# Token lists of a mixture-of-experts layer inverted in two passes instead of one

## The reference, cut to what matters

```
x  = x + layernorm(attention(layernorm(x)))
xf = layernorm(x)                                   # 4096 x 256
probs = softmax(xf @ gate_w.T); topw, topi = top_k(probs, 2)
topw  = topw / topw.sum()
y  = ffn(xf, shared) + sum over e of ffn(xf, expert[e]) * weight of e (0 where e was not chosen)
x  = x + layernorm(y)
ffn(x, g, u, d) = (silu(x @ g.T) * (x @ u.T)) @ d.T  # g, u: 704 x 256; d: 256 x 704
```

## Time and profile before

| | us |
|---|---|
| median of 3 runs | 857.32 (856.37 to 857.96) |
| the profiled execution | 857.45 |
| its span in the trace | 855.7 |

### The profile page before, as it was taken

How to read it: one execution, slowest core, us unless ns; L and a number is a source line. 1 busy time by engine, 2 the same in 40 slices (tenths; PEclk the granted TensorE clock), 3 DMA queues, 4 the chain that set the end, 5 groups by cost and what they waited for, 6 DMA issues and landing times.

```text
span 855.7 us, 21069 instructions
## 1 busy us (share of the span) xinstructions
PE 786.6 (92%) x6583; PEld 643.3 (75%) x6592; DVE 586.6 (69%) x1591; ACT 484.8 (57%) x1068; POOL 291.6 (34%) x316
## 2 busy tenths in 40 slices
PE   6889999999999998666899999999999999999991
PEld 2447777777777776544788888888888888888880
DVE  6668889898988888894887444555555555555553
ACT  2264848485757675422566555565656565656562
POOL 3011010101010100062265555555555555555542
PEclk9999999999999999997999999999999999999996
DMA  4104334443535252502245545646463646464733
GB/s 191 50 25 179 112 142 112 152 125 144 145 121 152 101 156 74 148 1 71 50 68 77 100 76 73 123 76 145 72 148 70 148 69 148 68 146 68 147 42 96
DMA packets 102691, 90.10 MB, mean 105 GB/s; under 512 B 63760, under 2 KB 94224, under 8 KB 101456
## 3 DMA queue, kind: packets, MB, share of 16 engines
q1 hardware_dynamic: 87648, 68.45, 27.7%
q0 software_dynamic: 14976, 20.78, 16.0%
HBM read 48.70 MB, written 27.39 MB: 89 GB/s over the span
## 4 chain that ended last, share of the span: by engine, by line
PE 68%; DVE 17%; ACT 6%; issue 4%; DMA 3%; POOL 1%; ACTq 0%; SPq 0%; DVEq 0%; POOLq 0%
PE ps L911 39%; PE ps L926 18%; PE ps L991 3%; DVE wgu L1286 3%; PE ps L1023 3%; DVE hf L1226 2%; ACT wgu L771 2%; PE ps L985 2%; DVE wdn L1286 1%; DVE st L1402 1%; DVE st L1206 1%; DVE wdn L1535 1%; PE ps L952 1%; DVE hT L1236 1%; ACT silu L723 1%
## 5 line engine op out<-in xcount | busy, mean ns | idle before, releaser
L911 PE MATMUL ps<-xhl,wgu 128*128 128x256 f16 x3102 | 386.3, 274 | 13.1 <-DMA xhl<-attw 6.5
L911 PEld LDWEIGHTS ps<-xhl,wgu 128*128 (+1 forms) x3102 | 302.9, 98 | 57.6 <-issue 10.4
L1226 DVE SCALAR_TENSOR_TENSOR hf<-ps,sc,silu 128x256 f32<-128x256 f32 x330 | 159.6, 484 | 187.5 <-ACT silu L723 148.2
L926 PE MATMUL ps<-wdn,hT 128*128 (+1 forms) x1870 | 253.7, 274 | 11.3 <-DVE hT L1236 8.9
L723 ACT ACTIVATE silu<-ps,sc 128x256 f32<-128x256 f32 x275 | 130.4, 474 | 234.1 <-PE ps L911 211.4
L926 PEld LDWEIGHTS ps<-wdn,hT 128*128 128x128 f16 x1870 | 182.4, 98 | 37.1 <-DVE hT L1236 6.3
L672 POOL DMA_INDIRECT acc_d<-ysb,gst x78 | 129.2, 1657 | 44.5 <-POOL gst L668 30.9
L605 POOL TENSOR_TENSOR rstd<-ve,mhalf 128x4 f32<-128x4 f32 (+1 forms) x32 | 30.7, 960 | 297.5 <-DVE ve L1211 276.2
L1236 DVE TENSOR_TENSOR hT<-hf,hT 128x256 f16<-128x256 f32 x275 | 115.1, 418 | 1.7
L737 ACT CAST hT<-hf 128x256 f16<-128x256 f32 x275 | 109.8, 399 | 10.2 <-DVE hf L1226 8.4
L661 POOL DMA_INDIRECT attw<-xn_d,gst x78 | 80.4, 1031 | 44.5 <-POOL gst L657 32.6
(11 more groups left out here) (241 smaller groups left out, 775.2 us busy)
## 6 DMA issues: line engine op xcount, KB each, us to landing
wgu<-in_gu SPq DMA_DIRECT2D x8, 1408.0 KB, 6.0
att<-in_x SPq DMA_DIRECT2D x16, 512.0 KB, 5.5
wdn<-in_dn SPq DMA_DIRECT2D x8, 768.0 KB, 8.1
x_d<-att SPq DMA_DIRECT2D x8, 512.0 KB, 2.9
xn_d<-wgu SPq DMA_DIRECT2D x8, 512.0 KB, 3.3
acc_d<-ysb SPq DMA_DIRECT2D x16, 256.0 KB, 3.1
att<-x_d SPq DMA_DIRECT2D x8, 512.0 KB
att<-acc_d SPq DMA_DIRECT2D x7, 512.0 KB
```

Source lines behind the costliest of these rows:

```text
L911: ins = te.matmul(o, slot_gu(slot, hw, k, j), x(hx, k), start=(n == 0), stop=(n == len(TERMS) - 1))
L926: ins = te.matmul(y_bank(u, tt), h(hh), slot_dn(slot, c, hw), start=(c == 0 and n == 0 and tt == 0), stop=(c == FC - 1 and n == 1 and tt = ...
L1226: v.scalar_tensor_tensor(out=hf[lo:P, c % 2 * TW:(c % 2 + 1) * TW], in0=up, scalar=scale_of(slot, 1, lo, P), in1=silu[lo:P, c % 2 * TW:(c ...
```

## The change

The lists of the eight constant tiles (16 columns) are inverted first, in TAIL. The lists of the others (62 columns) are inverted in routed tiles 0 to 3: VectorE makes eight groups of column one-hots at the positions HOT_AT of the routed tiles' chunks, TensorE multiplies two chunks later, and `route_indices(1)` follows. A position is six times the tile plus the chunk.

- Every expert's list now starts at a fixed place, so that the 16 columns need no counts. Ranks come from matmuls over prefixes (`ranks`: 28 matmuls for the first 28 blocks, 11 for the last 4) in place of L1048, L1049 and the eight scans.
- Place one-hots (`one_lo`) are one instruction of 1024 columns for four blocks, all on VectorE, without the token's number; all eight groups are kept in `att`. Column one-hots (`one_hi`) are made by two instructions, a comparison and a product with the token's number: 896 and 128 columns for the first pass, 496 columns in each of eight groups for the second.
- `route_weights` is a step of its own; its first part moves behind `rows2` and `logits` of batch 7. `route_positions` is done in two parts.
- Counts, segments, `route_order` and `route_table` move behind the first pass's indices.
- SP stores the routing weights in two parts, and loads expert 8's weights after tile 4's transposes and the second pass's last matmul, since `att` holds the place one-hots till then. The preparation of expert 8 moves from positions 17 to 32 to positions 26 to 37.
- GpSimd waits for the second part of `idx` before the gather of tile 8; ScalarE and TensorE wait for `eid` before tile 8 and no longer before tile 0.

```
 LAST_ORDER: ("route_norm", 0) now ahead of ("route_top1", 0); ("route_weights", 0) behind ("logits",); ("route_slots", 0) ahead of ("D", 11)
+TAIL = [("G", 0), ("route_positions", 0), ("H", 0), ("route_norm", 1), ("G", 1), ("route_top1", 1), ("G", 2), ("H", 1), ("D", 0), ("route_top2", 1),
+        ("one_lo", 0), ("G", 3), ("H", 2), ("route_slots", 1), ("D", 1), ("route_weights", 1), ("one_lo", 1), ("one_hi", 0), ("G", 4), ("H", 3),
+        ("D", 2), ("invert", 0), ("route_positions", 1), ("one_lo", 2), ("one_lo", 3), ("invert", 1), ("G", 5), ("H", 4), ("D", 3), ("invert", 2),
+        ("one_lo", 4), ("one_lo", 5), ("invert", 3), ("invert", 4), ("G", 6), ("one_lo", 6), ("one_lo", 7), ("one_hi", 1), ("invert", 5),
+        ("invert", 6), ("invert", 7), ("route_indices", 0), ("H", 5), ("D", 4), ("route_counts",), ("G", 7), ("H", 6), ("D", 5),
+        ("route_segments",), ("G", 8), ("H", 7), ("D", 6), ("route_order",), ("G", 9), ("H", 8), ("D", 7), ("G", 10), ("H", 9), ("D", 8),
+        ("route_table",), ("G", 11), ("H", 10), ("D", 9), ("H", 11), ("D", 10), ("D", 11)]
+PREP_AT = ((0, 2, 4, 6, 7, 8, 9, 11, 13, 15), (26, 27, 28, 29, 30, 31, 32, 34, 35, 37))
+PREP_STEPS = (("max", 0), ("max", 1), ("max", 2), ("diag", 0), ("spread", 0), ("scale", 0), ("prep", 0), ("prep", 1), ("prep", 2), ("prep", 3))
+HOT_AT = (1, 3, 5, 10, 12, 14, 16, 18)
+LATE |= {divmod(at, FC): ("one_hi", 0, g) for g, at in enumerate(HOT_AT)}
+LATE |= {divmod(HOT_AT[-1] + 3, FC): ("indices", 0, 0)}
+INVERT_AT = {divmod(at + 2, FC): g for g, at in enumerate(HOT_AT)}
...
 # SP, in the loop over the routed tiles
+                if i == 5:
+                    sp.wait_ge(rest_used, OHG)
+                    sp.dma_start(last_gu, gu_in[E]).then_inc(last_loaded, 16)
+                    sp.dma_start(last_dn, dn_in[E]).then_inc(last_loaded, 16)
...
 # TensorE
+            def ranks(n):
+                t0, t1 = PART[n]
...
+                te.matmul(dst, upper16, m16[:, E * t0:E * t1], start=True, stop=False)
+                for b in range(PART_B[n][0]):
+                    te.matmul(dst.rearrange("p (t e) -> p t e", e=E), ones16[:, :], each(bsum16[:, E * b:E * b + E], t1 - t0), start=False, stop=False)
+                for t in range(t0, t1 - 1):
+                    ins = te.matmul(dst[:, E * (t + 1 - t0):].rearrange("p (t e) -> p t e", e=E), ones16[:, :], each(m16[:, E * t:E * t + E], t1 - 1 - t),
+                                    start=False, stop=(t == t1 - 2))
...
+            def invert(n, g):
+                pe.wait_ge(onehot_lo_made, g + 1)
...
+                for h in range(OHB):
+                    for m in range(2):
+                        hi = oh_first[:, m, OHB * g + h, :] if n == 0 else oh_rest[g % 2][:, m, h, :]
+                        ins = te.matmul(inverted(n), oh_lo[g][:, m, h, :], hi, start=(g == 0 and h == 0 and m == 0), stop=(g == OHG - 1 and h == OHB - 1 and m == 1))
+                ins.then_inc(rest_used if n else first_used, 1)
...
 # VectorE
+            def one_hi(dst, lo, hi, c0, c1, made):
+                shape = [P, 2, hi - lo, c1 - c0]
...
+                rl(v.tensor_tensor(dst, h4, c4, ALU.is_equal))
+                v.tensor_tensor(dst, dst, t4, ALU.mult).then_inc(made, 1)
+            def one_lo(g):
+                shape = [P, 2, OHB, P]
...
+                v.tensor_tensor(oh_lo[g], l4, i4, ALU.is_equal).then_inc(onehot_lo_made, 1)
```

More of the change, by code:

```diff
@@ L77 @@
[L77 to L82, removed]
@@ L204, in build @@
         last_gu, last_dn = att[:, 0:KD * GU], att[:, KD * GU:KD * GU + FC * D]
[L207 to L211, removed]
+        routes = wdn[:, (E - 1) * SLOT_DN:E * SLOT_DN].bitcast(F32)
+        r_p, r_t, r_o1, r_o2, r_c, r_x = (routes[:, NTB * E * n:NTB * E * (n + 1)] for n in range(6))
+        route_rest = spare[:, 2 * KD * S + 2 * NT * D:SLOT_GU].bitcast(F32)
@@ L221, in build @@
[L221 to L226, removed]
+        STATIC = E * TT
@@ L1026, in _ @@
                         ins.then_inc(att_done, 1)
+                if kind == "route_slots":
+                    ranks(step[1])
                 if kind == "turn2" and b in PE_SECOND:
@@ L1044, in _ @@
                 if kind == "route_slots":
-                    pe.wait_ge(m_made, 2)
-                    x2_ready(pe, B - 1)
-                    te.matmul(att_ps[0][:, 0:256], upper[:, :], r_m, start=True, stop=True)
-                    te.matmul(att_ps[0][:, 256:512], ones[:, :], r_m, start=True, stop=True).then_inc(counted, 1)
+                    ranks(step[1])
+                if kind == "route_counts":
+                    pe.wait_ge(logits_made, B)
+                    for b in range(B):
+                        ins = te.matmul(att_ps[3][:, E * b:B * E].rearrange("p (t e) -> p t e", e=E), ones16[:, :], each(bsum16[:, E * b:E * b + E], B - b),
+                                        start=(b == 0), stop=(b == B - 1))
+                    ins.then_inc(counted, 1)
                 if kind == "route_order":
@@ L1053, in _ @@
                 if kind == "invert":
-                    for h in range(OHB):
-                        j = OHB * step[1] + h
-                        pe.wait_ge(onehot_made, step[1] + 1)
-                        pe.wait_ge(onehot_lo_made, POOL_H * step[1] + max(1, h - (OHB - POOL_H) + 1))
-                        for m in range(2):
-                            ins = te.matmul(att_ps[1][:, 0:NCOL], oh_lo[step[1] % OHR][:, m, h, :], oh_hi[step[1]][:, m, h, :],
-                                            start=(j == 0 and m == 0), stop=(j == NTB - 1 and m == 1))
-                    ins.then_inc(onehot_used, 1)
-            pe.wait_ge(eid_made, 1)
+                    invert(0, step[1])
             def routed(i, r, slot, before, later=None):
@@ L1335, in route @@
                     first_of(o2, m2)
-                    v.tensor_tensor(mm, o1, o2, ALU.add).then_inc(m_made, 1)
+                    rl(v.tensor_tensor(mm, o1, o2, ALU.add))
+                    sums = bsum16[:, E * PART_B[n][0]:E * PART_B[n][1]]
+                    with nc.allow_low_precision(reason="whole numbers up to 4"):
+                        v.tensor_reduce(sums.rearrange("p (b e) -> p b e", e=E), mm.rearrange("p (b t e) -> p b e t", t=NT, e=E), AX.X, ALU.add).then_inc(m_made, 1)
+                if kind == "route_weights":
                     rl(v.tensor_tensor(ms, m1, m2, ALU.add))
@@ L1461, in _ @@
                     ffn_step(kind, step[1], 2 * B - 2, 0)
[L1462 removed]
+                if kind in ("route_norm", "route_top1", "route_top2", "route_weights", "route_positions"):
                     route(kind, step[1])
[L1464 to L1476 removed]
+                if kind == "one_lo":
+                    if step[1] == 0:
+                        dve.wait_ge(rows2_hi, B)
+                        dve.wait_ge(x2_stored, 16 * B)
+                    one_lo(step[1])
@@ new lines, in _ @@
+                if kind == "one_hi":
+                    if step[1] == 0:
+                        c3 = col16.rearrange("p (i h) -> p i h", h=TT)
+                        for h in range(TT):
+                            ins = v.tensor_scalar(c3[:, 0:E, h], expert_at, 1.0 / P, float(h), ALU.mult, ALU.add)
+                        rl(ins)
+                    one_hi(oh_first[:, :, PART[step[1]][0]:PART[step[1]][1], :], PART[step[1]][0], PART[step[1]][1], 0, STATIC, first_hi_made)
+                if kind == "route_indices":
+                    route_indices(0)
@@ L1577, in lay_out @@
                     prep(s, n, *stage)
+                if kind == "one_hi":
+                    wait(dve, rest_used, n - 1)
+                    one_hi(oh_rest[n % 2], OHB * n, OHB * (n + 1), STATIC, NCOL, rest_hi_made)
+                if kind == "indices":
+                    route_indices(1)
             def ml(ins, b, n):
```

230 lines of the change are left out of this document (129 added, 101 removed), and 6 rows, old and new, of the table LAST_ORDER.

## The result

| | before | after |
|---|---|---|
| median of 4 runs, us | 857.01 (856.37 to 857.96) | 864.6 (863.71 to 865.52) |
| profiled execution, us | 857.45 | 863.71 |
| its span, us | 855.7 | 861.9 |

The account below looks back on a forecast made before the run. DVE was taken to set the pace in the tail until the token lists stand, PE in the routed tiles. 857.45 - 5.8 (tail) + 3.5 (routed tiles) = 855.15, adjusted to the median: forecast 855.0 us, range 850 to 861.

Parts of the forecast that it names:

- The tail: From batch 7's end to tile 0's first matmul: tile 0 starts 5.8 us sooner, at 396.5, bounds 393.5 and 400.
- Rows ready earlier, tile 0 no longer waits: Start of tile 0: first lists at 379.1, rows at 388.9, PE's 6.5 us wait for transposed rows gone.
- I take 1.14 for `one_lo`: Place one-hots on DVE: 1.14 us per 1024-column instruction, one element a cycle; 0.55 or 1.4 were the alternatives.
- H7 at 383.2 to 383.9: Shared expert in the tail: DVE's step H7 was walked to run from 383.2 to 383.9 us, then order until 387.3.
- tile 0 starts at 396.5: End of the tail: PE free at 395.4, plus 1.1 us for slow matmuls; bounds 393.5 and 400.
- The walk: Step-by-step count of the tail along DVE's and PE's queues, giving tile 0's start.
- The point at 348.12 becomes 350.4: DVE's last softmax block in the tail: moving the weights' first part costs 2.15 us and one 0.1 us wait.
- Give-back 3.5, bounds 0.5 to 8: Routed tiles 0 to 6: second-pass matmuls and DVE stalls, less the cold start, lose 3.5 us net.
- the cold start: Tile 0's first 36 matmuls: following other work, they fall from 5.57 to 3.9 us, gaining 1.65.
- C: Rival, routed tiles 0 to 5: DVE overload makes PE wait, give-back 8 us, tail 1 us worse, 860.5; chance 0.2.
- D: Rival, tail: not shorter because PE runs slowly through most of it, tile 0 at 400, time 858.5; chance 0.13.
- Expert 8's load: 0, bounds 0 and 4: Weight load for expert 8, now starting at position 20.5, needed behind 26: costs 0 us, bounds 0 and 4.

Follow-up runs that it names:

- Number 3: The changed kernel with `route_order` moved ahead of H7 and D6 in the tail; 864.25 us, ratio 1.0065 to the kernel before.
- number 11: The changed kernel measured once more, unchanged, on another chip; 867.56 us, ratio 1.0117 to the kernel before.
- number 6: The changed kernel with the routing weights' first part back in its old place behind `route_top2`; 861.42 us, ratio 1.0043 to the kernel before.
- number 2: The changed kernel with both spreads, scale and pieces one chunk later; 861.7 us, ratio 1.0026 to the kernel before.
- number 5: The changed kernel with one of eight second-pass groups, expert 8's load kept at the changed kernel's place; 858.51 us, ratio 1.0013 to the kernel before.
- Number 1: The changed kernel with only the first of eight second-pass groups, which also released expert 8's load earlier; 865.82 us, ratio 1.0073 to the kernel before.
- 4: The changed kernel with 16 filler matmuls of 256 columns ahead of each of the two late spreads; 866.85 us, ratio 1.0073 to the kernel before.
- 8: The changed kernel with the edits of numbers 2, 3 and 6, plus 66 filler matmuls in the tail; 852.9 us, ratio 0.9949 to the kernel before.
- 9: Number 8 without its 66 filler matmuls; 851.71 us, ratio 0.994 to the kernel before.
- 10: Number 8 with `route_table` earlier, two second-pass one-hot groups made in the tail, the other six repositioned; 850.23 us, ratio 0.9913 to the kernel before.
- 7: The changed kernel with the edits of numbers 2 and 3 together; 854.68 us, ratio 0.996 to the kernel before.

## Why the prediction was wrong, step by step

Two terms of the sum failed. The tail was to gain 5.8 us and gained 3.0, most of that by luck; the routed tiles were to give back 3.5, at most 8, and gave back 9.8. The second turned the sign: its stalls were put too small, and the low clock behind a stalled spread was put at nothing.

- **"Rows ready earlier, tile 0 no longer waits": right.** First copy of `idx` at 380.48 (forecast 379.1, 392.60 before), no wait for `xhl<-attw`, 36 matmuls in 4.12 us (forecast 3.9). The forecast's 3.9 counts from start to start and its 5.57 to the end of the last matmul, so that its gain of 1.65 was 0.2 too large; like for like it is the 1.45 that was measured.
- **"I take 1.14 for `one_lo`": right.** 4.54 us for four. The half of the rule in the Trainium skill (Vector Engine (DVE) Microarchitecture Reference, 5.1 Performance modes) on which the sum rested, that one element read again and again brings one element a cycle, holds for 1024 columns as for 624; two elements a cycle would, by an estimate from that, have given 2.3 us for four.
- **"H7 at 383.2 to 383.9" and "tile 0 starts at 396.5": failed.** H7 came at 388.05, tile 0 at 400.25, just outside the upper bound of 400. The walk followed DVE and PE, but not ScalarE's queue: Silu of H7 stands behind the output of tile 14, this waits for D5, and D5 stands behind a G7 at 1.2 GHz. Number 3 and the table in number 11 show it: with the order steps in that pause H7 starts at 386.64, and tile 0 starts some 3 us earlier behind the lists. The tail gained 3.0 us (forecast 5.8), of which 1.7 are the gate group at full clock, which owes nothing to the change; in number 11 nothing is gained.
- **"The point at 348.12 becomes 350.4": the cost was right, the point 0.9 too late.** It came at 349.54. The move cost 2.15 us (forecast 2.25; number 6), 0.94 was lost far ahead of it, and the gate group at full clock gave 1.7 back. PE's pause before D10, forecast as 3 us and more, was 3.72. From this point to the lists it took 30.9 us where the walk had 28.7: the rank matmuls held DVE for 1.71 (forecast 0.5), the first Silu for 1.47 (forecast 0.8).
- **"Give-back 3.5, bounds 0.5 to 8": failed; it measured 9.8.** By terms: the matmuls cost 1.8 (8 groups at 0.22 to 0.23; forecast 2.2), the cold start gave back 1.45 (forecast 1.65), idle time grew by 4.9 (forecast 3.6). The stall at the first spread was 2.13 (forecast 1.5) and at the second 2.07 (forecast 2.2). What the sum did not have at all is the clock behind them. From 417.77 to 423.15, 34 down and gate matmuls took 5.38 us where 3.72 is their time at 2.4 GHz (0.66 + 1.31 + 0.44 + 1.31), and from 468.05 to 474.08 6.03 us instead of 4.38: 3.3 us for both. Some 1.2 us of PE's busy time are not put down to a row; an estimate puts 0.8 of it on the pauses: a group of 12 is busy for 1.47 where the next can start after 1.31, so that each pause leaves 0.16 of an overlap unused, and after has 11 pauses in this stretch for 6 before. The sum of these is 1.8 - 1.45 + 4.9 + 3.3 + 1.2 = 9.8. Number 11 against after shows the clock as a cost of its own (3.71 and 5.38 us for the same matmuls behind the same wait), number 2 that the wait for the diagonal was the cause of most of it (6.9 us of the stage), number 5 that the second pass was what made the first diagonal late (a wait of 0.85 without it). The second diagonal is as late without the second pass (2.07 in number 5): that wait comes from the three maxima in a row, as forecast. The bound of 8 was a bound of stalls alone; the other profiles with these steps (3, 6, 11) gave back 7.7 to 9.3. Tile 6's yw came 83.8 us behind tile 0's start, where 76 to 77 were forecast.
- **Rivals.** C's mechanism, DVE's overload in tiles 0 to 5, is what happened. Its place (the spreads) was right and its price (8) too small, again for lack of the clock. The result lies above its 860.5 by 1.8 in the tail, 1.8 in the tiles and the 0.94 ahead of both, less the 1.5 of the later tiles. D's slow groups came, and tile 0 at its 400. By the Trainium skill (TensorE: Matmul & The Clock Gate, Part 1) the low clock is the default and activity releases it. PEclk of 0.51 at 418 to 420, right behind a 2.13 us wait, agrees with that; 1.00 behind number 11's 2.14 shows that it doesn't say which wait will cost. The low clock was priced in the tail and not at the pauses which the same text had forecast in tiles 1 and 5.
- **"Expert 8's load: 0, bounds 0 and 4": right for after,** where nothing waited for it. Number 1 shows the risk: released 9 us sooner, it stopped ScalarE's output for 4.78 us. By the Trainium skill (DMA: Bandwidth & Descriptors, Queues, rings and completion order) the engines switch between issuers packet by packet, so a large load only shares with the scatters. If it was the scatter that the output waited for, 4.78 us is what that sharing came to in number 1; no row names what ended the wait.

**Still open.** Why 0.94 us were lost ahead of anything that the change touches: PEclk from 50 to 60 us was 0.83 in after and in numbers 2, 4, 8, 9, 10 and 11, and 1.00 in before and in numbers 1, 3, 5, 6 and 7, although the work there is the same. It goes with the loss: the mark ahead of `route_weights` stands at 327.07 to 328.19 in the first and at 325.77 to 326.63 in the others, changed kernels among both. Why after is at 1.0086 on one chip and 1.0117 on another. Why the last 29 tiles took 1.5 us less. And the rest of the 1.2 us of busy time named above.

## What to carry to other kernels

- A stall of PE has two prices: its length and the low clock that may follow it (here 1.66 us, behind six of ten waits of some 2.1 us). Price both wherever the forecast itself puts such a wait between matmuls, and first try to move the waiting instruction one slot back: here that was worth 0.6% of the whole, at no cost.
- The same instructions can take one of several lengths from profile to profile. Before two profiles are compared, look for a group that both have and the change doesn't touch; compare short stretches, in as many profiles as there are.
- When a walk goes by two engines' queues, walk the third as well. An instruction that waits in order on an engine with little to do (here ScalarE's output copy) holds back the critical one behind it.
- Work that doesn't fit into one stage may fit in the pauses of the one ahead of it; look where the engine that has to do it idles while another sets the pace.
